# A ninth block in a mixture-of-experts kernel: laying the code behind each "is there a further block?" so that no jump is taken

## The chip, the cores and the metric

The kernel runs on one core of one Trainium2 chip. The time is the device time of one execution in microseconds (us). Five engines run their own instruction streams and meet by semaphores: PE (TensorE, matrix products), DVE (VectorE), ACT (ScalarE), POOL (GpSimd) and SP (SyncE, which here only starts transfers).

## The reference

32 samples of 64 tokens x 256 channels each go through the feed-forward net of one of eight experts, the one that the sample's index names; then come the residual and a layer norm.

```python
Wi_b = Wi[expert_idx]            # 256 x 1024 per sample
Wo_b = Wo[expert_idx]            # 1024 x 256 per sample
h = gelu(einsum('bsh,bhi->bsi', x, Wi_b) + bi_b, exact)
o = einsum('bsi,bih->bsh', h, Wo_b) + bo_b
r = o + x
mu = mean(r); var = mean(square(r - mu))
y = (r - mu) * rsqrt(var + 1e-12) * g_b + be_b
```

With the inputs used the experts have 3, 4, 8, 4, 4, 4, 4 and 1 samples.

## The kernel before

The kernel sorts the samples by expert at run time and works in *blocks* of four samples of one expert (256 tokens). The first eight blocks are one for each expert; an expert with more than four samples gets further blocks behind them. So the number of blocks `n`, read by each engine from a small table (`entry`, L183), lies between `MIN_BLOCKS` = 8 and `MAX_BLOCKS` = 15. Here it is 9: the expert with eight samples has a second block.

For a block, PE multiplies the tokens by the first weights into `preact` (`first_product`, four parts), ACT applies gelu in place and writes the upper half of each number (`h_hi`), DVE the lower half (`h_low`, L602); PE then forms the output sums in `sums_ps` from the halves (`second_product`, four parts: 0 and 1 for the first tile of 128 tokens, 2 and 3 for the second). The weights are split into halves in the same way, `wo_r` for the second ones (ACT L452, DVE `wo_low` L590, in two pieces). Each product of split numbers is three matmuls: L734 or L758, L707 and L708. DVE adds the residual and centres (`centre`, L609 to L615; `centre_last` for the very last tile), ACT sums the squared deviations (`deviations`, L485), POOL takes the root (L376), DVE scales (`finish`, L639), and SP, for the last quarter ACT, stores.

The engines work staggered. PE's step t does the first product of block t between the parts of the second product of block t - 1; DVE's step t holds the second centring of block t - 2 (at its start) and the first of block t - 1. Nothing but each engine's own order and its semaphore waits sets the order of work.

Steps that always occur stand in a row. For the others each engine has a nest of questions: `from_block` (PE and SP) and `with_next` (DVE, ACT, POOL). A question "n > t?" is a compare-and-branch. In before, on yes the code goes on right behind it, with the step of the further block, the next question and all that is nested in it; on no it jumps to the Else part, which holds the end of the work. The Else parts of the inner questions stand ahead of those of the outer ones, so a whole nest lies between a question and its Else. At the end of an Else there is a short jump over the Else parts further out. The questions here are "n > 8?" (yes) and "n > 9?" (no). SP's end (L326) issues the last stores and waits for all of them (L333) ahead of its last jump; behind it lies the exit (DRAIN and semaphore, L60 in the trace), where the engines wait for each other.

Of the kernel before, what the change touches and what calls it, by code (L numbers as in the profile page):

```python
# [18 lines left out]
def expert_ffn(nc, xr, xt, idx, wi, wo, par, out):  # L19
# [13 lines left out]
    MIN_BLOCKS = E  # L33
# [26 lines left out]
    with ctx:  # L60
# [200 lines left out]
        def store(eng, t, slots):  # L261
            rows = samples(eng, t)
            for j in slots:
                eng.wait_ge(y_ready, 2 * t + j // 2 + 1)
                eng.dma_start(out[bass.ds(rows[j], 1), :, :].rearrange("o s h -> (o s) h"), slot(t, j)).then_inc(
                    stored[t % X_RING], 16)

        def from_block(eng, n, t, iteration, end):

            if t == MAX_BLOCKS:  # L270
                end(t)
                return
            with eng.If(n > t):
                iteration(t, t + 1)
                from_block(eng, n, t + 1, iteration, end)
                eng.nop()
            with eng.Else():
                end(t)
                eng.nop()

        def with_next(eng, n, t, iteration, end):

            if t + 1 == MAX_BLOCKS:
                iteration(t, False)
                end(t + 1)
                return
            with eng.If(n > t + 1):
                iteration(t, True)
                with_next(eng, n, t + 1, iteration, end)
                eng.nop()  # L290
            with eng.Else():
                iteration(t, False)
                end(t + 1)
                eng.nop()

        @block.sync
        def _(sp):
# [39 lines left out]
            for t in range(1, MIN_BLOCKS - 2):  # L337
                iteration(t, True)
            from_block(sp, n, MIN_BLOCKS, lambda t, _: iteration(t - 2, True), end)

        @block.gpsimd
        def _(pool):
# [55 lines left out]
            for t in range(MIN_BLOCKS - 1):  # L398
                iteration(t, True)
            with_next(pool, n, MIN_BLOCKS - 1, iteration, end)  # L400

        @block.scalar
        def _(act):
# [118 lines left out]
            for t in range(MIN_BLOCKS - 1):  # L522
                iteration(t, True)
            with_next(act, n, MIN_BLOCKS - 1, iteration, end)

        @block.vector
        def _(dve):
# [149 lines left out]
            for t in range(MIN_BLOCKS - 1):  # L677
                iteration(t, True)
            with_next(dve, n, MIN_BLOCKS - 1, iteration, end)

        @block.tensor
        def _(pe):
# [89 lines left out]
            for t in range(MIN_BLOCKS):  # L772
                iteration(t, True)
            from_block(pe, n, MIN_BLOCKS, iteration, end)


# [30 lines left out]
```

## Time and profile before

| | us |
|---|---|
| median of 3 runs | 131.44 (130.99 to 132.53) |
| the profiled execution's own time | 131.33 |
| its span, first to last instruction | 129.4 |
| PE busy | 114.2 (88%) |
| DVE busy | 100.3 (78%) |
| ACT busy | 96.2 (74%) |
| POOL busy | 69.3 (54%) |

The profile is one execution. Times in it count from the start of its span. A "q" behind an engine's name means its sequencer, which carries out waits, jumps and the issue of transfers.

### The profile page before, as it was taken

How to read it: one execution, taken by the hardware profiler on the slowest of the kernel's cores; microseconds unless marked ns; L12 is line 12 of the kernel's file. 1: busy time of each engine (PE TensorE's matmuls, PEld its weight loads, DVE VectorE, ACT ScalarE, POOL GpSimd, SP SyncE). 2: the span in 40 equal slices, each digit the busy share in tenths (PEclk: the TensorE clock that was granted, in tenths of full speed). 3: DMA queues.
4: the chain of work that ended last, by engine and by line, in shares of the span. 5: the costliest groups of instructions: out<-in, count | busy, mean ns of one | idle time of the engine just before them, and what ended most of it. 6: DMA issues, size and time to landing. Idle time of an engine off the chain costs nothing.

```text
span 129.4 us, 2750 instructions
## 1 busy us (share of the span) xinstructions
PE 114.2 (88%) x880; PEld 110.6 (85%) x880; DVE 100.3 (78%) x191; ACT 96.2 (74%) x186; POOL 69.3 (54%) x84
## 2 busy tenths in 40 slices
PE   6979960999999999999999999999999996968910
PEld 6758851999999999999999999999999996957900
DVE  3500569959899999989998998999899658946370
ACT  3104399999999899989989998998999638860100
POOL 4041048138298749839883983888398417202220
PEclk9976998599999999999999999999999999999997
DMA  2889999999479939966992997599582210110111
GB/s 72 285 182 372 394 329 401 387 392 372 174 213 403 356 90 363 390 225 196 398 382 72 318 388 271 183 400 352 130 314 77 68 46 3 41 45 5 46 41 41
DMA packets 21144, 29.81 MB, mean 230 GB/s; under 512 B 2112, under 2 KB 11328, under 8 KB 21120
## 3 DMA queue, kind: packets, MB, share of 16 engines
q1 hardware_dynamic: 18208, 23.84, 54.1%
q10 hardware_dynamic: 2048, 3.35, 8.2%
q0 software_dynamic: 864, 2.36, 4.8%
q8 instruction: 9, 0.15, 0.5%
q14 instruction: 15, 0.12, 0.3%
HBM read 27.18 MB, written 2.36 MB: 228 GB/s over the span
## 4 chain that ended last, share of the span: by engine, by line
PE 64%; DVE 14%; issue 7%; DMA 6%; ACT 3%; SPq 2%; POOL 1%; DVEq 0%; POOLq 0%
PE sums_ps L758 12%; PE sums_ps L708 11%; PE sums_ps L707 11%; PE preact L734 9%; PE preact L708 9%; PE preact L707 9%; DMA xT_in<-x_columns 6%; DVE wo_r L590 4%; DVE h_lo L602 3%; DVE wi_lo L584 3%; PE preact L685 2%; DVE r L609 2%; SPq L246 2%; DVE centred L615 1%; POOL rstd L376 1%
## 5 line engine op out<-in xcount | busy, mean ns | idle before, releaser
L758 PE MATMUL sums_ps<-wo_r,h_lo 128*128 128x256 f32 x144 | 41.5, 288 | 6.0 <-DVE wo_r L590 4.5
L708 PE MATMUL sums_ps<-wo_r,h_hi 128*128 128x256 f32 x144 | 41.1, 286 | 0.1
L707 PE MATMUL sums_ps<-wo_r,h_hi 128*128 128x256 f32 x144 | 41.1, 285 | 0.0
L734 PE MATMUL preact<-xT_r,wi_lo 128*128 128x256 f32 x128 | 36.4, 284 | 0.4 <-DVE xT_r L595 0.4
L707 PE MATMUL preact<-xT_r,wi_hi 128*128 128x256 f32 x128 | 36.1, 282 | 0.0
L708 PE MATMUL preact<-xT_r,wi_hi 128*128 128x256 f32 x128 | 36.0, 281 | 0.0
L758 PEld LDWEIGHTS sums_ps<-wo_r,h_lo 128*128 128x128 f32 x144 | 27.6, 192 | 6.7 <-issue 5.2
L468 ACT ACTIVATE preact<-preact,params 128x256 f32<-128x256 f32 x64 | 25.8, 441 | 3.1 <-PE preact L708 3.0
L708 PEld LDWEIGHTS sums_ps<-wo_r,h_hi 128*128 128x128 f32 x144 | 27.7, 192 | 0.3 <-issue 0.3
L707 PEld LDWEIGHTS sums_ps<-wo_r,h_hi 128*128 128x128 f32 x144 | 27.6, 192 | 0.0
L258 POOL DMA_INDIRECT xs<-x_rows,row_of x18 | 21.1, 1175 | 9.2 <-issue 9.1
L366 POOL TENSOR_TENSOR xs<-xs,params 128x256 f32<-128x256 f32 x18 | 18.9, 1068 | 12.6 <-DMA params<-vectors 7.7
L584 DVE TENSOR_TENSOR wi_lo<-wi_in,wi_hi 128x1024 fp32r<-128x1024 f32 x16 | 20.4, 1273 | 6.7 <-ACT wi_hi L434 6.7
L602 DVE TENSOR_TENSOR h_lo<-preact,h_hi 128x512 fp32r<-128x512 f32 x36 | 24.6, 682 | 0.8 <-ACT h_hi L477 0.6
L734 PEld LDWEIGHTS preact<-xT_r,wi_lo 128*128 128x128 f32 x128 | 24.2, 189 | 0.8 <-DVE xT_r L595 0.8
L707 PEld LDWEIGHTS preact<-xT_r,wi_hi 128*128 128x128 f32 x128 | 24.2, 189 | 0.0
L708 PEld LDWEIGHTS preact<-xT_r,wi_hi 128*128 128x128 f32 x128 | 24.1, 188 | 0.0
L376 POOL TENSOR_TENSOR rstd<-var_eps,minus_half 128x1 f32<-128x1 f32 x18 | 21.4, 1190 | 3.5 <-DVE var_eps L630 2.0
L373 POOL TENSOR_SCALAR var_eps<-deviation 128x1 f32<-128x1 f32 x17 | 6.5, 380 | 29.9 <-ACT squares L485 29.7
L477 ACT ACTIVATE h_hi<-preact 128x512 fp32r<-128x512 f32 x36 | 21.6, 600 | 1.1
L590 DVE TENSOR_TENSOR wo_r<-wo_in,wo_r 128x1024 fp32r<-128x1024 f32 x18 | 21.9, 1215 | 0.3 <-ACT wo_r L452 0.3
L452 ACT ACTIVATE wo_r<-wo_in 128x1024 fp32r<-128x1024 f32 x18 | 18.9, 1051 | 0.0
(67 smaller groups left out, 109.7 us busy)
## 6 DMA issues: line engine op xcount, KB each, us to landing
wo_in<-w_out SPq DMA_DIRECT2D x8, 1024.0 KB
wi_in<-w_in SPq DMA_DIRECT2D x7, 1024.0 KB, 8.5
params<-vectors SPq DMA_DIRECT2D x9, 388.0 KB, 6.8
y_rows<-xs SPq DMA_DIRECT2D x35, 64.0 KB, 2.2
xT_in<-x_columns SPq DMA_DIRECT2D x34, 64.0 KB, 5.9
wi_in<-w_in ACTq DMA_DIRECT2D x4, 512.0 KB, 5.3
wo_in<-w_out ACTq DMA_DIRECT2D x2, 512.0 KB, 8.9
xs<-x_rows,row_of POOLq DMA_INDIRECT x18, 5.8
```

The lines of the kernel that those rows point to most:

```text
L258: pool.indirect_dma_start(xs[:, t % X_RING, tile, :], None, xr.rearrange("o s h -> (o s) h"), rows_of(t, tile)).then_inc(x_loaded[t % X_RI ...
L366: nc.gpsimd.tensor_tensor(xs[:, t % X_RING, tile, :], xs[:, t % X_RING, tile, :], row(0, t), ALU.add).then_inc(xs_ready, 1)
L376: nc.gpsimd.tensor_tensor(rstd[:, tile:tile + 1], var_eps[:, tile:tile + 1], minus_half[:, :], ALU.pow).then_inc(rstd_ready, 1)
L468: done = nc.scalar.activation(to, pre, ACT.Gelu, bias=bias[:, c:c + 1])
L477: nc.scalar.activation(h_hi[:, t % 2, 2 * q:2 * q + 2, :].rearrange("p c n -> p (c n)"), preact[:, q, :], ACT.Copy).then_inc(h_hi_done, 1)
L584: nc.vector.tensor_tensor(flat(wi_lo, t % 2, wi_piece(piece)), flat(wi_in, t % WI_RING, wi_piece(piece)), flat(wi_hi, t % 2, wi_piece(piec ...
L590: nc.vector.tensor_tensor(wo_r[:, t % 2, a:b, 1, :], wo_in[:, t % WO_RING, a:b, :], wo_r[:, t % 2, a:b, 0, :].bitcast(FP32), ALU.subtract) ...
L602: nc.vector.tensor_tensor(lo, preact[:, q, :], hi.bitcast(FP32), ALU.subtract).then_inc(h_lo_done, 1)
L707: nc.tensor.matmul(columns, weight, parts[:, 0, :], start=False, stop=False)
L708: return nc.tensor.matmul(columns, weight, parts[:, 1, :], start=False, stop=stop)
L734: nc.tensor.matmul(columns, wi_lo[:, t % 2, c, k, :], xT_r[:, t % 2, k, 0, :], start=(k == 0), stop=False)
L758: nc.tensor.matmul(columns, h_lo[:, t % 2, c, tokens], wo_r[:, t % 2, c, 0, :], start=(c == 0), stop=False)
```

## The change

For the first question behind the minimum (n > 8) nothing changes. From the next one on the question is put the other way round: "n < t + 1?", and what stands right behind it is the end of the work; the further block and the nest of questions stand in the Else. The same holds for `with_next`, where the short part is the step without a successor and the end. The work of each branch is the same.

```diff
         def from_block(eng, n, t, iteration, end):
 
             if t == MAX_BLOCKS:
                 end(t)
-                return
-            with eng.If(n > t):
-                iteration(t, t + 1)
-                from_block(eng, n, t + 1, iteration, end)
-                eng.nop()
-            with eng.Else():
-                end(t)
-                eng.nop()
+            elif t == MIN_BLOCKS:
+                with eng.If(n > t):
+                    iteration(t, t + 1)
+                    from_block(eng, n, t + 1, iteration, end)
+                    eng.nop()
+                with eng.Else():
+                    end(t)
+                    eng.nop()
+            else:
+                with eng.If(n < t + 1):
+                    end(t)
+                    eng.nop()
+                with eng.Else():
+                    iteration(t, t + 1)
+                    from_block(eng, n, t + 1, iteration, end)
+                    eng.nop()
...
         def with_next(eng, n, t, iteration, end):
 
             if t + 1 == MAX_BLOCKS:
                 iteration(t, False)
                 end(t + 1)
...
+            else:
+                with eng.If(n < t + 2):
+                    iteration(t, False)
+                    end(t + 1)
+                    eng.nop()
+                with eng.Else():
+                    iteration(t, True)
+                    with_next(eng, n, t + 1, iteration, end)
+                    eng.nop()
```

The rows below are those of the order of instructions, in which plain semaphore waits and register moves have no row; row numbers in the text count an engine's rows from its stream's start. The first place is DVE at its question "n > 9?", row 145 in both kernels. Before, the step for a further block stands behind it, and the code for exactly nine blocks begins at row 444:

```order
L287 COMPARE_AND_BRANCH
L609 SCALAR_TENSOR_TENSOR r,total<-sums_ps,xs 128x256
L612 TENSOR_SCALAR less_mean<-total 128x1
L615 SCALAR_TENSOR_TENSOR centred<-r,less_mean,params 128x256
L602 TENSOR_TENSOR h_lo<-preact,h_hi 128x512
L590 TENSOR_TENSOR wo_r<-wo_in,wo_r 128x4x256
L584 TENSOR_TENSOR wi_lo<-wi_in,wi_hi 128x1024
...
L287 UNCONDITIONAL_BRANCH
L609 SCALAR_TENSOR_TENSOR r,total<-sums_ps,xs 128x256
L612 TENSOR_SCALAR less_mean<-total 128x1
L615 SCALAR_TENSOR_TENSOR centred<-r,less_mean,params 128x256
```

After, the step without a successor stands right behind the question (no `wi_lo`), and its end is the jump in row 176:

```order
L305 COMPARE_AND_BRANCH
L627 SCALAR_TENSOR_TENSOR r,total<-sums_ps,xs 128x256
L630 TENSOR_SCALAR less_mean<-total 128x1
L633 SCALAR_TENSOR_TENSOR centred<-r,less_mean,params 128x256
L620 TENSOR_TENSOR h_lo<-preact,h_hi 128x512
L608 TENSOR_TENSOR wo_r<-wo_in,wo_r 128x4x256
L620 TENSOR_TENSOR h_lo<-preact,h_hi 128x512
...
L657 SCALAR_TENSOR_TENSOR xs<-centred,rstd,params 128x256
L305 UNCONDITIONAL_BRANCH
L627 SCALAR_TENSOR_TENSOR r,total<-sums_ps,xs 128x256
```

With nine blocks DVE used to jump from row 145 to 444; now it goes straight on, and jumps at row 176, behind its last work, to row 470 and from there over the code for eight blocks to the end. ACT, POOL and PE are laid in the same way.

The second place is the end of SP's stream. Before, the last stores for nine blocks end in row 555, reached by a jump from row 164; row 556 jumps over the code for exactly eight blocks (557 to 589) to the exit:

```order
L273 COMPARE_AND_BRANCH
L197 TENSOR_LOAD table
...
L273 UNCONDITIONAL_BRANCH
L189 TENSOR_LOAD table
...
L265 DMA y_rows<-xs 64x256
L277 UNCONDITIONAL_BRANCH [waits stored4,stored5,stored3,stored1,stored2,stored0]
L273 UNCONDITIONAL_BRANCH
L189 TENSOR_LOAD table
```

After, those stores stand behind the question in row 164:

```order
L282 COMPARE_AND_BRANCH
L189 TENSOR_LOAD table
...
L265 DMA y_rows<-xs 64x256
L282 UNCONDITIONAL_BRANCH [waits stored4,stored5,stored3,stored1,stored2,stored0]
L197 TENSOR_LOAD table
...
L285 UNCONDITIONAL_BRANCH [waits stored4,stored5,stored3,stored1,stored2,stored0]
L285 UNCONDITIONAL_BRANCH x5
L274 UNCONDITIONAL_BRANCH
L189 TENSOR_LOAD table
```

The jump that carries the last wait for the stores stands at row 197 and leads to row 552, over the code for ten to fifteen blocks; 552 jumps on to the exit.

## Rows read from the trace of the kernel before

**Rows 1.** The page: busy time of each engine, the chain by engine
```profile
PE 114.2 (88%) x880; PEld 110.6 (85%) x880; DVE 100.3 (78%) x191; ACT 96.2 (74%) x186; POOL 69.3 (54%) x84
...
PE 64%; DVE 14%; issue 7%; DMA 6%; ACT 3%; SPq 2%; POOL 1%; DVEq 0%; POOLq 0%
```

**Rows 2.** Timeline, 102 to 109 us: start, us, engine, line, [idle before, releaser]
```profile
102.27 0.29 PE L708 MATMUL sums_ps<-wo_r,h_hi 128*128 128x256 f32 x1
...
104.84 0.42 DVE L609 SCALAR_TENSOR_TENSOR r<-sums_ps,xs 128x256 f32<-128x256 f32 x1 [2.47 <-issue]
...
105.50 0.51 ACT L485 ACTIVATE squares<-r,less_mean 128x256 f32<-128x256 f32 x1 [2.88 <-DVE less_mean L612]
...
106.50 1.22 DVE L590 TENSOR_TENSOR wo_r<-wo_in,wo_r 128x1024 fp32r<-128x1024 f32 x1
...
106.56 0.28 PE L708 MATMUL preact<-xT_r,wi_hi 128*128 128x256 f32 x1
...
107.87 0.36 PE L758 MATMUL sums_ps<-wo_r,h_lo 128*128 128x256 f32 x1 [1.03 <-DVE wo_r L590]
```

**Rows 3.** DVE, ACT: the question, the first instruction behind it (ns, start us)
```profile
L287 DVEq COMPARE_BRANCH  x1: 67/67/67, 101.9 to 101.9; - x1
L287 ACTq COMPARE_BRANCH  x1: 50/50/50, 102.0 to 102.0; - x1
...
L607 DVEq EVENT_SEMAPHORE  x1: 21/21/21, 104.8 to 104.8; - x1
...
L484 ACTq EVENT_SEMAPHORE  x1: 17/17/17, 104.8 to 104.8; - x1
```

**Rows 4.** Instruction packets, 102.9 to 103.0 us, then 105.4 to 105.6
```profile
q14 instruction: 2, 0.02, 61.7%
...
q14 instruction: 2, 0.02, 22.7%
```

**Rows 5.** PE: its question; its instruction packets, 117.1 to 117.3 us
```profile
L273 PEldq COMPARE_BRANCH  x1: 3482/3482/3482, 113.0 to 113.0; - x1
...
q8 instruction: 1, 0.02, 37.4%
```

**Rows 6.** Timeline, 114.5 to 120 us, of PE and DVE
```profile
114.97 0.28 PE L708 MATMUL sums_ps<-wo_r,h_hi 128*128 128x256 f32 x1
...
115.36 0.42 DVE L609 SCALAR_TENSOR_TENSOR r<-sums_ps,xs 128x256 f32<-128x256 f32 x1 [1.80 <-PE sums_ps L708]
...
116.62 0.36 PE L758 MATMUL sums_ps<-wo_r,h_lo 128*128 128x256 f32 x1 [1.37 <-DVE r L609]
...
117.02 1.22 DVE L590 TENSOR_TENSOR wo_r<-wo_in,wo_r 128x1024 fp32r<-128x1024 f32 x1
...
118.39 0.36 PE L758 MATMUL sums_ps<-wo_r,h_lo 128*128 128x256 f32 x1
...
119.30 0.28 PE L707 MATMUL sums_ps<-wo_r,h_hi 128*128 128x256 f32 x1
...
119.67 0.39 PE L708 MATMUL sums_ps<-wo_r,h_hi 128*128 128x256 f32 x1
```

**Rows 7.** SP: its question, the first instruction behind it (ns, start us)
```profile
L273 SPq COMPARE_BRANCH  x1: 53/53/53, 92.9 to 92.9; - x1
...
L189 SPq TENSOR_LOAD <-table x1: 311/311/311, 98.0 to 98.0; - x1
```

**Rows 8.** SP at the end: last wait, two jumps, exit (ns, start us)
```profile
L279 SPq EVENT_SEMAPHORE  x1: 1596/1596/1596, 126.9 to 126.9; - x1
...
L277 SPq COMPARE_BRANCH  x1: 43/43/43, 128.5 to 128.5; - x1
...
L273 SPq COMPARE_BRANCH  x1: 38/38/38, 128.7 to 128.7; - x1
...
L60 SPq DRAIN  x1: 55/55/55, 129.1 to 129.1; - x1
L60 SPq EVENT_SEMAPHORE  x1: 17/17/17, 129.3 to 129.3; - x1
```

More of the change, by code:

```diff
@@ L285, in with_next @@
                 end(t + 1)
[L286 to L294, printed above, removed]
+            elif t + 1 == MIN_BLOCKS:
+                with eng.If(n > t + 1):
+                    iteration(t, True)
[7 more added lines that the diff above has]
+                with eng.If(n < t + 2):
+                    iteration(t, False)
+                    end(t + 1)
+                    eng.nop()
+                with eng.Else():
+                    iteration(t, True)
+                    with_next(eng, n, t + 1, iteration, end)
+                    eng.nop()
         @block.sync
```

## Prediction

> **What bounds the kernel now.** I read the page first: PE is busy for 114.2 of 129.4 us and carries 64% of the chain that ended last, DVE 14%, and 7% is "issue", time in which an engine waited for nothing that the profile shows [rows 1]. An edit that only moves code can change nothing but such issue time and PE's idle time, so I looked for both behind the questions. The eight experts make nine blocks with these inputs (one expert has eight samples, the others at most four), so "more than 8?" is answered yes and "more than 9?" no. In before the no of the second question is a jump over the code of six further blocks, on each engine.
>
> *DVE and ACT.* DVE asks at 101.9 and executes its next instruction at 104.8; ACT asks at 102.0 and goes on at 104.8 [rows 3]. That is 2.9 and 2.8 us for one jump. What DVE goes on to is the residual sum of block 6 (L609), with 2.47 us idle ahead of it and "issue" as the reason [rows 2]. PE had handed over that sum long before: its last matmul for it starts at 102.27 [rows 2]. In the same stretch two packets of the instruction queue start at 102.9 to 103.0 us, and two more at 105.4 to 105.6 [rows 4]: the code at the far end was not on the engine, was fetched after the jump, and its continuation after the landing.
>
> *PE.* Its sequencer runs ahead of its array, asks at 113.0 and sits in that instruction for 3.48 us [rows 5]. The last matmul of block 7 starts at 114.97, the first one behind the jump at 116.62 [rows 6]. The timeline names DVE's sum as the releaser; that sum frees only the second token tile, and the matmul at 116.62 writes the first, so the jump is what ended last.
>
> *SP.* It asks at 92.9 and goes on at 98.0, 5.1 us later [rows 7], with a 1 MB weight load issued just ahead. Nothing on the chain waits for it there. At the end SP waits for the last stores, 1.6 us from 126.9, takes a jump at 128.5 and a second at 128.7, and reaches its exit at 129.1 and 129.3 [rows 8]. Both of these jumps are short, at most over the code for exactly eight blocks.
>
> **The change part by part.** No instruction of the work is added or removed; the order of work is the same on each engine. What changes is where the taken jumps are.
>
> *Removed, DVE and ACT behind block 7's step.* DVE can take the sum once PE's matmuls are done. Elsewhere it starts 0.39 us behind the start of PE's last matmul (114.97 to 115.36, [rows 6]), so here at 102.27 + 0.39 = 102.66, not 104.84: 2.18 us earlier. The work behind it follows in the same order: DVE's low half of the second weights (L590) starts at 104.3, not 106.50, and ends by 105.5. PE wants that half right behind its matmul of 106.56, and gets it only for 107.87, with 1.03 us idle [rows 2]. Start to start that is 1.31 us where matmuls follow each other at 0.12 us (for instance 118.39 to 119.30 with seven between, [rows 6]). So PE gains 1.31 - 0.12 = **1.19 us**. The other 1.0 us of DVE's 2.18 is slack. ACT's wait of 2.88 us for DVE's mean [rows 2] goes with it, and its own jump of 2.8 us, which lay inside that wait, too.
>
> *Removed, PE behind block 8's step.* The first matmul of the last output product could start 1.5 us earlier (116.62 less 114.97 and 0.12). The second group, at 118.39, waits for the other weight half, which DVE starts at 117.02 and which takes 1.22 us, until 118.24 [rows 6]; DVE began that run at 115.36 on PE's finished sum, before PE was through the jump. So this jump is hidden behind DVE and its removal gives **0**. If DVE's run were shorter it would give up to 1.5 us; what is late next is the weight half in either case. But the jump has a second effect: one more packet of PE's instruction queue starts at 117.1 to 117.3 [rows 5], and at 119.67 a matmul comes 0.37 us behind its predecessor of 119.30 [rows 6]. I read this as code behind the landing that arrived late. Falling through, it arrives in its turn: **0.25 us** gained, 0 if my reading is wrong.
>
> *Removed, SP and POOL.* SP's 5.1 us go, but the stores there feed nothing but the ring of six, and POOL's jump comes while it waits for ACT's deviations in any case: 0. If SP's stores had been late for the ring, POOL's loads would show it; there are none left to make after block 8.
>
> *Sum up to the last store:* -1.19 - 0.25 = -1.44 us, on DVE, ACT and PE alike, since the tail (sum, deviations, root, scale, store) follows PE's last matmul one by one. Bounds: -1.19 to -2.2 (DVE's whole gain).
>
> *Added: the last block's code is now the first branch, so its end jumps over the code of six further blocks.* In before this end lay one short jump from the exit. On SP the new jump spans 355 rows of the order of instructions (197 to 552); the one that cost 5.1 us in before spans 359 (164 to 523). PE, DVE, ACT and POOL get such a jump too, but each has done its last work before the last store lands at 128.5 [rows 8], so their jumps run ahead of SP's. SP takes it *after* its wait for the last stores, and all engines wait for SP. Nothing hides it. Price: no row shows a far jump with idle DMA queues. Below lies the short jump, 0.2 us from 128.5 to 128.7 [rows 8]; above lies SP's own 5.1 us. The nearest are DVE's 2.9 and ACT's 2.8, with light DMA traffic; SP's 5.1 came behind a full megabyte of weights, and at the end the queues are empty. I take 2.85, less the 0.2 that the short jump cost: **+2.65 us**.
>
> *Added, possibly: the code behind the exit.* The profiled execution took 131.33 us for a span of 129.4, so 1.93 us lie around it. DVE's and ACT's landings at 104.8 are followed by packets 0.6 to 0.8 us later [rows 3, 4], so what stands behind SP's landing is not there yet. From packet to use it takes 1.9 us (102.9 to 104.8), so that code is usable some 2.6 us behind the landing, and SP wants it after 0.8 (128.5 to 129.3, [rows 8]): up to 1.8 us late, an estimate. Whether that falls inside the measured time no row shows. Between 0 and 1.8 I take 0.4, near the lower end, since the span itself does not contain it.
>
> **Sum:** 131.33 - 1.44 + 2.65 + 0.4 = 132.94 us. The profiled execution lies 0.11 below the median of 131.44, which runs from 130.99 to 132.53; I say **133.0 us**.
>
> [...] In before, far jumps cost 2.8 to 5.1 us [rows 3, 7]. [...]
>
> **The rivals.** *Faster: the last jump costs nothing.* The condition is that the far code is on SP already, for instance fetched in its 1.6 us of waiting. For it: every other jump in the program gets cheaper. Against: ACT and DVE waited the full time though they too had idle stretches, and SP can't know its target before it executes the jump. It decides if the price falls below 1.44. Time: 131.44 - 1.44 = 130.0. Chance 14%.
>
> *Slower still: the code behind the exit counts in full.* 133.0 + 1.4 = 134.4. Chance 18%.
>
> *The gain does not come.* DVE's earlier start meets another wait, ACT's first activations of block 8, and PE stays at 107.87; against it, these depend on PE's own product, ready at 104. Time: 131.44 + 2.65 + 0.4 = 134.5. Chance 8%.
>
> *Gain and loss cancel*, since with idle queues the fetch is quicker: a price of 1.4 gives 131.4. Chance 10%. That the code is not moved as said is excluded by the order of instructions.
>
> **How the numbers follow.** The forecast (132.4 to 133.6) has 50%. One per cent, about what a measurement of this kernel can tell from no change, is 1.3 us: 130.1 to 132.75. Of the forecast's 50% some 33 lie above 132.75 and 17 below. Slower: 33 + 18 + 8 = 59%. Same: 17 + 10 = 27%. Faster: 14%. The range leaves out the faster rival and the top of the slower ones: 131.2 to 134.5.
>
> **What the profile after would show.** DVE's sum of block 6 at about 102.7 and no "issue" idle there; PE's idle of 1.03 us gone; PE from block 7 to block 8 without a gap at the question, but then about 1.9 us idle before the second group; SP's last wait ending at about 127.1 (128.5 - 1.44); and between the start of SP's last jump pair and its exit some 3.3 us where 0.6 stood. If that last gap is short the prediction is wrong on the fast side; if the span has grown by 1.2 and the time by 2.5 or more, the code behind the exit counted.

## The result, and the profile after

The changed kernel takes 134.36 us in the median of 4 runs (134.22 to 134.99); the kernel before 131.22 in the runs beside it. The ratio is 1.0262, with a 95% interval of 1.0193 to 1.0332: **slower by 2.6%**, where 133.0 us, 1.2% over the median shown before, was forecast. The direction was right; the loss forecast was half of the one that came. A run more than 1.5% above the fastest of the same kernel counts as slow: the ratios here and below leave slow runs out, the medians keep them, and the profiles of three experiments (28 instructions more, DVE and ACT, DVE only) are of slow runs.

The page of the changed kernel: span, busy time of each engine, the instruction packets of the four engines other than PE, and the chain by engine.

```profile
span 132.3 us, 2754 instructions
...
PE 112.2 (85%) x880; PEld 109.9 (83%) x880; DVE 99.8 (75%) x191; ACT 96.6 (73%) x186; POOL 69.2 (52%) x84
...
q14 instruction: 14, 0.11, 0.3%
...
PE 73%; DMA 6%; DVE 4%; ACT 4%; issue 3%; SPq 2%; POOL 1%; DVEq 0%; POOLq 0%
```

The span is 2.9 us longer, PE's busy time is no longer than before [rows 1], and the chain has less "issue" in it (3% for 7%). So the loss is not in the work. The timeline around block 7 and 8, as before (all lines lie 18 further down, so L627 is the old L609, L608 the old L590, L503 the old L485):

```profile
102.52 0.29 PE L726 MATMUL sums_ps<-wo_r,h_hi 128*128 128x256 f32 x1
...
102.92 0.42 DVE L627 SCALAR_TENSOR_TENSOR r<-sums_ps,xs 128x256 f32<-128x256 f32 x1 [0.30 <-PE sums_ps L726]
...
103.58 0.51 ACT L503 ACTIVATE squares<-r,less_mean 128x256 f32<-128x256 f32 x1 [0.72 <-DVE less_mean L630]
...
104.58 1.22 DVE L608 TENSOR_TENSOR wo_r<-wo_in,wo_r 128x1024 fp32r<-128x1024 f32 x1
```

This answers to [rows 2]. DVE takes its sum 0.40 us behind the start of PE's last matmul for it, where it had sat 2.47 us with the reason "issue". ACT's deviations follow at 103.58 and the weight half starts at 104.58; in before they came at 105.50 and 106.50. PE's matmul L758, now L776, has no idle row here any more. At the start of the last output product, the stretch of [rows 6]:

```profile
114.36 0.42 DVE L627 SCALAR_TENSOR_TENSOR r<-sums_ps,xs 128x256 f32<-128x256 f32 x1 [1.80 <-PE sums_ps L726]
...
116.02 1.22 DVE L608 TENSOR_TENSOR wo_r<-wo_in,wo_r 128x1024 fp32r<-128x1024 f32 x1
...
117.38 0.36 PE L776 MATMUL sums_ps<-wo_r,h_lo 128*128 128x256 f32 x1 [1.73 <-DVE wo_r L608]
```

PE passes its question (at 112.0) without a gap and then waits 1.73 us for DVE's weight half, ahead of the second group; the forecast had said about 1.9.

SP's end in the changed kernel answers to [rows 8]: its last wait, the long jump, the short jump, and the exit (duration in ns as min/median/max, then first and last start in us).

```profile
L284 SPq EVENT_SEMAPHORE  x1: 1603/1603/1603, 125.5 to 125.5; - x1
...
L282 SPq COMPARE_BRANCH  x1: 38/38/38, 127.1 to 127.1; - x1
...
L274 SPq COMPARE_BRANCH  x1: 38/38/38, 129.7 to 129.7; - x1
...
L60 ACTq DRAIN  x1: 8/8/8, 128.6 to 128.6; - x1
L60 SPq DRAIN  x1: 58/58/58, 132.0 to 132.0; - x1
L60 SPq EVENT_SEMAPHORE  x1: 17/17/17, 132.2 to 132.2; - x1
```

The last store has landed at 127.1, 1.4 us earlier than in before. Then 2.5 us pass from the long jump to the short one (127.14 to 129.68), and another 2.3 from the short one to DRAIN (129.7 to 132.0), where 0.2 and 0.4 stood in before. The other engines are at the exit long before: ACT, the last of them, at 128.6. The profile lists packets of the kind "instruction" on two queues, q8 (9 packets, 0.15 MB together, about 17 KB each, in both kernels) and q14 (14 packets, 0.11 MB together, about 8 KB each, in the changed one). In before one of q8 starts at 113.94, 0.97 us behind PE's jump of 112.97; of q14 two start at 102.94, behind DVE's jump of 101.91 and ACT's of 102.02, one at 101.62, behind POOL's of 100.32, and one at 96.33, behind SP's of 92.92. In the changed kernel, which takes none of these jumps, q14 has no packet from 87.5 to 98.5 us nor from 98.6 to 124.6, and q8 none from 98.7 to 118.8. I therefore read q8 as PE's and q14 as that of the other four. The place where an engine goes on behind a jump is called its landing here. The packets that matter in the two gaps start at 127.9 to 128.3 us (two, of which one may be another engine's) and at 130.2 to 130.3; one more, at 129.3, follows ACT's landing of 128.4:

```profile
q14 instruction: 2, 0.02, 11.0%
...
q14 instruction: 1, 0.01, 35.4%
```

**The wait for the second packet is what the forecast had too small.** The target of the short jump behind the landing lies in a packet of its own; that packet starts 0.55 us behind the landing, and SP waits for it in full, inside the span.

### The profile page after: what moved, and what is told of

Same layout as the page of the kernel before. It is cut to its first block, busy times and chain, and to the rows that moved or that the text cites. A ratio compares the mean times of both kernels' runs of the same rounds, so it can differ in the third digit from the quotient of the medians.

```text
span 132.3 us, 2754 instructions
## 1 busy us (share of the span) xinstructions
PE 112.2 (85%) x880; PEld 109.9 (83%) x880; DVE 99.8 (75%) x191; ACT 96.6 (73%) x186; POOL 69.2 (52%) x84
## 4 chain that ended last, share of the span: by engine, by line
PE 73%; DMA 6%; DVE 4%; ACT 4%; issue 3%; SPq 2%; POOL 1%; DVEq 0%; POOLq 0%
PE sums_ps L776 13%; PE sums_ps L726 12%; PE sums_ps L725 12%; PE preact L752 11%; PE preact L726 11%; PE preact L725 11%; DMA xT_in<-x_columns 6%; PE preact L703 2%; DVE wo_r L608 2%; SPq L246 2%; ACT preact L486 1%; POOL rstd L394 1%; ACT h_hi L495 1%; ACT wo_r L470 1%; ACT wi_hi L452 1%
## 5 line engine op out<-in xcount | busy, mean ns | idle before, releaser
L776 PE MATMUL sums_ps<-wo_r,h_lo 128*128 128x256 f32 x144 | 41.2, 286 | 5.2 <-DVE wo_r L608 5.2
L776 PEld LDWEIGHTS sums_ps<-wo_r,h_lo 128*128 128x128 f32 x144 | 27.5, 191 | 5.6 <-issue 5.6
L486 ACT ACTIVATE preact<-preact,params 128x256 f32<-128x256 f32 x64 | 25.8, 441 | 3.7 <-PE preact L726 3.5
L384 POOL TENSOR_TENSOR xs<-xs,params 128x256 f32<-128x256 f32 x18 | 19.9, 1128 | 12.4 <-DMA params<-vectors 7.5
L258 POOL DMA_INDIRECT xs<-x_rows,row_of x18 | 20.0, 1111 | 9.5 <-issue 9.4
L602 DVE TENSOR_TENSOR wi_lo<-wi_in,wi_hi 128x1024 fp32r<-128x1024 f32 x16 | 19.8, 1240 | 6.0 <-ACT wi_hi L452 6.0
L608 DVE TENSOR_TENSOR wo_r<-wo_in,wo_r 128x1024 fp32r<-128x1024 f32 x18 | 21.9, 1217 | 0.5 <-ACT wo_r L470 0.5
```

The costliest lines, as they stand in the source:

```text
L258: pool.indirect_dma_start(xs[:, t % X_RING, tile, :], None, xr.rearrange("o s h -> (o s) h"), rows_of(t, tile)).then_inc(x_loaded[t % X_RI ...
L384: nc.gpsimd.tensor_tensor(xs[:, t % X_RING, tile, :], xs[:, t % X_RING, tile, :], row(0, t), ALU.add).then_inc(xs_ready, 1)
L486: done = nc.scalar.activation(to, pre, ACT.Gelu, bias=bias[:, c:c + 1])
L608: nc.vector.tensor_tensor(wo_r[:, t % 2, a:b, 1, :], wo_in[:, t % WO_RING, a:b, :], wo_r[:, t % 2, a:b, 0, :].bitcast(FP32), ALU.subtract) ...
L776: nc.tensor.matmul(columns, h_lo[:, t % 2, c, tokens], wo_r[:, t % 2, c, 0, :], start=(c == 0), stop=False)
```

## The experiments

All kernels compute the whole result. In the experiments by engine both forms of the nest stand side by side; `from_block_yes` and `with_next_yes` are the nest of the kernel before. The same code ahead of the questions ends at different times from run to run (see the end). So the table gives for each profiled execution also two stretches that start at DVE's question "n > 9?": one to SP's first jump behind its last wait, which holds the gain, and one to SP's exit, which holds gain and loss. They are taken from the trace at its full resolution, so they can differ by 0.1 from the rounded times.

| kernel, changed nest on | median, us | ratio to before (95%) | DVE's question to SP's jump behind its last wait, us | DVE's question to exit, us |
|---|---|---|---|---|
| before (none) | 131.22 | | 26.6 | 101.9 to 129.3: 27.4 |
| after (all five) | 134.36 | 1.026 (1.019 to 1.033) | 25.0 | 102.2 to 132.2: 30.0 |
| all but SP | 130.20 | 0.989 (0.983 to 0.995) | 24.9 | 101.6 to 127.8: 26.3 |
| SP only | 136.52 | 1.038 (1.032 to 1.044) | 26.6 | 103.2 to 134.6: 31.4 |
| all five, 58 instructions more | 131.57 | 1.004 (0.999 to 1.009) | 25.0 | 101.2 to 129.2: 28.0 |
| all five, 28 instructions more | 133.74 | 1.016 (1.011 to 1.021) | 25.0 | 103.3 to 133.2: 29.9 |
| all but SP and ACT | 130.14 | 0.991 (0.987 to 0.995) | 25.0 | 101.7 to 127.5: 25.8 |
| DVE and ACT | 130.98 | 0.991 (0.985 to 0.997) | 25.2 | 103.0 to 129.6: 26.6 |
| DVE only | 130.55 | 0.989 (0.984 to 0.995) | 25.4 | 101.9 to 128.1: 26.2 |
| PE only | 131.14 | 1.000 (0.995 to 1.004) | 26.3 | 103.2 to 130.3: 27.1 |

The first stretch repeats well: 25.0 in all three kernels with all five engines changed, 26.6 in both kernels in which the other four are as before. The median of before was 131.47 beside the first four experiments and 131.68 beside the last four.

### All but SP

```diff
-            from_block(sp, n, MIN_BLOCKS, lambda t, _: iteration(t - 2, True), end)
+            from_block_yes(sp, n, MIN_BLOCKS, lambda t, _: iteration(t - 2, True), end)
```

> SP alone keeps the nest of the kernel before; PE, DVE, ACT and POOL have the changed one. Theory (SP's two jumps behind its last wait carry the whole loss): from SP's last wait to its exit 0.6 us as before, the gain of 1.4 us stays, so 131.2 - 1.4 = 129.8 us. Rival (the long jumps of the other engines at their ends hold the exit too, or slow it): their jumps end before the last store lands, so if they matter the time stays above 131 us.

Measured: 130.20 us, faster than before by 1.1%. The loss was SP's. The forecast of 129.8 was 0.4 us too low, and the rival was half right, on a smaller scale than it said: SP's jump at 126.4 (L323) and its DRAIN at 127.0 are as quick as in before, but the exit itself comes only at 127.8.

```profile
L323 SPq COMPARE_BRANCH  x1: 43/43/43, 126.4 to 126.4; - x1
...
L305 ACTq COMPARE_BRANCH  x1: 38/38/38, 124.8 to 124.8; - x1
...
L296 ACTq COMPARE_BRANCH  x1: 38/38/38, 127.5 to 127.5; - x1
...
L60 SPq DRAIN  x1: 55/55/55, 127.0 to 127.0; - x1
L60 ACTq DRAIN  x1: 8/8/8, 127.7 to 127.7; - x1
L60 SPq EVENT_SEMAPHORE  x1: 17/17/17, 127.8 to 127.8; - x1
```

ACT takes its own long jump at 124.8, behind the issue of its store, lands at 127.5 and reaches the exit at 127.7. With SP's loss gone it is ACT that the others wait for, by 0.6 us. So of the engines' late jumps each counts as far as it ends behind the others.

### SP only

```diff
-            from_block(pe, n, MIN_BLOCKS, iteration, end)
+            from_block_yes(pe, n, MIN_BLOCKS, iteration, end)
...
-            with_next(dve, n, MIN_BLOCKS - 1, iteration, end)
+            with_next_yes(dve, n, MIN_BLOCKS - 1, iteration, end)
```

(the same for ACT and POOL)

> SP alone has the changed nest, the other four keep that of the kernel before. Theory: no gain ahead of the last store, and SP's two late jumps cost 2.4 and 1.85 us: 131.2 + 4.25 = 135.5 us. Rival (the loss belongs to the other engines): about 131.2 us.

Measured: 136.52 us; from the question to the exit 4.0 us more than before, against 4.25 expected. Both of SP's jumps wait again, with none of the other engines jumping at that time:

```profile
L282 SPq COMPARE_BRANCH  x1: 38/38/38, 129.8 to 129.8; - x1
...
L274 SPq COMPARE_BRANCH  x1: 38/38/38, 132.3 to 132.3; - x1
...
L60 SPq DRAIN  x1: 58/58/58, 134.4 to 134.4; - x1
```

From the long jump to the short one 2.5 us, from there to DRAIN 2.1. DVE, ACT and POOL have reached the exit by 128.3, so the packets of q14 behind that are SP's own. The one at 130.7 starts 0.9 us behind the long jump, the one at 132.8 starts 0.55 us behind the landing (windows 130.6 to 130.8 and 132.8 to 132.9 us):

```profile
q14 instruction: 1, 0.01, 13.1%
...
q14 instruction: 1, 0.01, 30.2%
```

The rival, a loss of the other engines, has fallen.

### The exit moved within its packet

The waits below stand in code that only ten or more blocks reach, so nothing of them runs; two of them make one instruction. They push the landing of the long jump and the exit behind it further on.

```diff
                 with eng.Else():
+                    if eng.engine == nc.sync.engine and t == MIN_BLOCKS + 1:
+                        for _ in range(116):
+                            eng.wait_ge(samples_ready, 1)
                     iteration(t, t + 1)
```

An *edge* is the place in SP's code where one packet ends and the next begins. The theory tested is that the short jump waits because an edge lies between the landing and its target. Its wait was priced at 1.85 us, the 2.30 from jump to DRAIN in the changed kernel (129.68 to 131.98) less the 0.45 of before (128.67 to 129.12). With landing and target in one packet 134.4 - 1.85 = 132.5 us was expected.

> The changed kernel with 58 wait instructions more in SP's code for ten and more blocks, which is never run here: landing and exit of the last two jumps lie 58 instructions further on. [...] Rival (any jump right behind a landing costs 2.3 us): 134.4 us.

> The same with 28 instructions. Control: if the edge lies at the exit or just ahead of it, as the packets of the kernel before suggest, landing and exit move but landing stays ahead of the edge and exit behind it: 134.4 us, as the changed kernel. If the edge lies just behind the landing, both are in one packet and it takes 132.5 us like the kernel with 58.

Measured: 131.57 us with 58 instructions, 133.74 with 28. SP's long jump, short jump and exit with 58:

```profile
L282 SPq COMPARE_BRANCH  x1: 38/38/38, 126.2 to 126.2; - x1
...
L274 SPq COMPARE_BRANCH  x1: 38/38/38, 128.9 to 128.9; - x1
...
L60 SPq DRAIN  x1: 13/13/13, 129.0 to 129.0; - x1
L60 SPq EVENT_SEMAPHORE  x1: 17/17/17, 129.2 to 129.2; - x1
```

The long jump costs what it did (126.2 to 128.9), the short one nothing: DRAIN follows at 129.0. With 28 the short jump waits 2.1 us as in the changed kernel:

```profile
L274 SPq COMPARE_BRANCH  x1: 38/38/38, 130.9 to 130.9; - x1
...
L60 SPq DRAIN  x1: 58/58/58, 133.0 to 133.0; - x1
```

So it is not the jump right behind a landing that costs, but a target in a packet that is not there. With 58 the packet that starts 0.55 us behind the landing, at 129.4, comes when SP is already through its exit, and nothing waits for it. Counted in the built program, the exit lies 50 instructions behind the landing. Moving both by 28 left the edge of a packet between them, so the edge lies more than 28 instructions behind the landing of the changed kernel; moving them by 58 carried both past it, so it lies 29 to 50 behind. This takes it to be one and the same edge in all three kernels; how many instructions a packet holds no run shows.

The median with 28 came out 0.7 us under the 134.4 that was expected, but its stretch from question to exit is that of the changed kernel (29.9 for 30.0). The median with 58 came out 0.9 us under the expected 132.5; from question to exit it is 2.0 less than in the changed kernel, for 1.85 expected. The rest lies ahead of the questions, where the code is the same; no run shows why. Against before the kernel with 58 gains nothing (1.004): the long jump still takes back what the early jumps give.

### All but SP and ACT

```diff
-            with_next(act, n, MIN_BLOCKS - 1, iteration, end)
+            with_next_yes(act, n, MIN_BLOCKS - 1, iteration, end)
```

on top of the kernel with SP as before.

> SP and ACT keep the nest of the kernel before; PE, DVE and POOL have the changed one. In the kernel with SP alone as before, ACT's own long jump, from 124.8 to 127.5, ends 0.6 us behind SP's arrival at the exit. Theory: with it gone the exit comes 0.6 us earlier, while ACT's jump behind block 7 (2.8 us at 102) is absorbed, since PE needs nothing of block 8's activations before block 8's own output product: 129.6 us. Rival (ACT's early jump now delays block 8, where it had lain under DVE's): 130.5 us or more.

Measured: 130.14 us, ratio 0.991. ACT now reaches the exit at 125.2, and SP's DRAIN is followed by the exit at once:

```profile
L60 ACTq DRAIN  x1: 378/378/378, 125.2 to 125.2; - x1
L60 SPq DRAIN  x1: 55/55/55, 127.3 to 127.3; - x1
L60 SPq EVENT_SEMAPHORE  x1: 17/17/17, 127.5 to 127.5; - x1
```

From question to exit it is 0.5 us shorter than with ACT's nest changed, for 0.6 expected, and the medians (130.20 and 130.14) don't separate the two. ACT's jump behind block 7 is there again, with 1.96 us idle, and is absorbed: DVE's sum of block 7 is still released by PE.

```profile
104.37 0.51 ACT L531 ACTIVATE squares<-r,less_mean 128x256 f32<-128x256 f32 x1 [1.96 <-issue]
...
108.19 0.42 DVE L655 SCALAR_TENSOR_TENSOR r<-sums_ps,xs 128x256 f32<-128x256 f32 x1 [0.48 <-PE sums_ps L754]
```

### DVE and ACT, DVE only, PE only

The edits are the same call replaced for the engines not named.

> DVE and ACT alone have the changed nest. Theory: the 1.19 us of PE's stall come back, ACT's long jump at its end holds the exit by some 0.6 us as in the kernel with SP alone as before: 131.3 - 1.19 + 0.6 = 130.7 us; PE still waits behind its question. Rival (PE's jump is on the path after all and takes the gain back): 131.3 us or more.

Measured: 130.98 us; 0.8 us less than before from question to exit, and 1.4 less up to SP's jump behind its last wait: ACT's long jump at the end takes back the rest. The rival has fallen.

> DVE alone has the changed nest. Theory (of all early jumps DVE's alone is on the path): the full 1.19 us, and no long jump at ACT's end: 130.1 us. Rival (ACT's jump of equal length lies behind DVE's and takes its place): ACT's deviations and activations start at 105 in either case and PE's gain is lost: 131.3 us.

Measured: 130.55 us, ratio 0.989; 1.2 us less than before from question to exit, as expected (1.19). ACT's jump does not take the place of DVE's. PE still has its own jump here:

```profile
115.50 0.36 PE L804 MATMUL sums_ps<-wo_r,h_lo 128*128 128x256 f32 x1 [1.64 <-issue]
...
115.64 1.22 DVE L636 TENSOR_TENSOR wo_r<-wo_in,wo_r 128x1024 fp32r<-128x1024 f32 x1
...
118.45 0.39 PE L754 MATMUL sums_ps<-wo_r,h_hi 128*128 128x256 f32 x1 [0.26 <-issue]
```

It idles 1.64 us ahead of 115.50 and nothing comes of it: the next group starts at 117.01, 0.15 us behind the end of DVE's half of 115.64, as it does in before (118.39 for 118.24). This idle row names "issue" where [rows 6] named DVE's sum, which bears out that there too the jump ended last. The late packet of PE is here as well, starting at 116.09: the matmul at 118.45 starts 0.53 us behind its predecessor, so 0.4 us are lost in this trace, where before lost 0.25. DVE's 1.2 us and these 0.4 add up to the 1.6 us that all five changed nests give.

> PE alone has the changed nest. Theory: its jump behind block 8 is hidden under DVE's run to the second weight half, so only the 0.25 us of the late instruction packet come back: 131.1 us, with the matmul group at 118.4 unmoved. Rival (PE's 3.5 us count): 129.9 us or less.

Measured: 131.14 us, ratio 1.000 (0.995 to 1.004). From question to exit 0.3 us less than before, as expected for the packet alone. PE's jump is gone, and its idle time stands ahead of the second group instead, together with the stall behind DVE's jump:

```profile
109.19 0.36 PE L804 MATMUL sums_ps<-wo_r,h_lo 128*128 128x256 f32 x1 [1.10 <-DVE wo_r L636]
...
118.36 1.22 DVE L636 TENSOR_TENSOR wo_r<-wo_in,wo_r 128x1024 fp32r<-128x1024 f32 x1
...
119.72 0.36 PE L804 MATMUL sums_ps<-wo_r,h_lo 128*128 128x256 f32 x1 [1.73 <-DVE wo_r L636]
```

The 1.10 us at 109.19 answer to the 1.03 of [rows 2], and the 1.73 us at 119.72 are where the 1.37 of [rows 6] went: PE waits about as long one group later. That group is unmoved, as expected: 16.56 us behind DVE's question, for 16.48 in before.

## Why the prediction was right and wrong

*Which jumps are on the path:* right. DVE's jump alone gives 1.2 us, for a term of 1.19. PE's gives 0, and its late packet 0.3 for 0.25 (0.4 once DVE's jump is gone). ACT's early jump gives nothing that shows: up to SP's jump behind its last wait it is 25.0 us with ACT as before and 24.9 with ACT changed, SP being as before in both. POOL's was not tried alone. SP's early 5.1 us were worth nothing, as said: with SP as before and all others changed the gain stands (24.9, for 25.0 with SP changed too).

*The gain up to the last store:* 1.44 us by the sum. SP's last wait ends at 127.1 for 128.5, 1.4 earlier; counted from DVE's question the changed kernel needs 25.0 us and before 26.6, so 1.6. The terms hold.

*The long jump of SP at the end:* 2.65 was forecast above the short one's cost; measured 2.5 from jump to jump (127.14 to 129.68) less 0.2, so 2.4. The row taken, DVE's and ACT's, was the right neighbour, and SP's own 5.1 us behind a megabyte of weights the wrong one. (In before its packet starts at 96.3, 3.4 us behind the jump of 92.9, where DVE's of 102.9 and those of SP's jumps at the end start 0.9 to 1.0 us behind. That the load held it up is likely, but no run leaves the load out.) The first rival, a free last jump, has fallen in four kernels: whenever SP has the changed nest, 2.5 to 2.7 us pass there. Nor was the code fetched during SP's wait for the last stores: with SP alone changed no packet of q14 starts from 109.1 to 130.6 us, and the one of 130.7 starts 0.9 us behind the jump.

*The code behind the landing:* **this is the step that failed.** I had priced a full wait for the packet behind the landing at up to 1.8 us and took 0.4 of it, because I placed that code behind the exit, outside the span. It lay ahead of the exit: the short jump's target, 50 instructions on, was across a packet's edge, and the jump cost 2.3 us for the 0.4 of before, 1.9 net, inside the span. The prediction's own sign says the same: from the start of SP's last jump pair to its exit it expected 3.3 us, and 4.8 passed, although the long jump itself took 0.3 less than its price.

With 1.9 in place of 0.4 the sum is 132.94 + 1.5 = 134.4 us, against 134.36 measured. That this fits to the tenth is partly luck. In the profiled execution the terms are -1.6, +2.4 and +1.85, and DVE's question comes 0.26 us later than in before, which no term had; 131.33 and these give 134.2, and 134.25 was measured. The second rival, with 134.4 us and 18%, names this mechanism and its price; its place was off by one jump.

The trace of before did not speak for 0.4. Its short jump needs 0.4 us to DRAIN [rows 8], where the kernel with 58 instructions more, whose landing and exit share a packet, needs 0.2. And a packet starts at 129.68, 0.56 us behind the DRAIN of before at 129.12, which is the distance measured behind SP's late landings (0.55). I read this now as an edge ahead of the exit in before too, with the packet behind it already there; no run tests that reading.

*What came out better:* laid for each engine by itself, the change is worth having for nine blocks. With the old nest on SP and the new one on the rest the kernel is 1.1% faster than before, and with DVE's alone changed it is too. All runs have nine blocks. With ten or more the changed nest jumps at "n > 9?" and at each further question but the last, where before jumps at the last alone; no run shows what that costs.

## What to carry to other kernels

A taken jump out of the code at hand cost 2.5 to 3.1 us on DVE, ACT and SP in these traces, 3.4 to 4.1 on PE, and 4.9 to 5.1 on SP just behind the issue of a large load. So ask of every branch not how often it is taken but what its engine is doing then: ahead of a wait that it has anyway, a jump was free (PE's: ratio 1.000 without it; SP's: 24.9 us to its last jumps with it, 25.0 without), and behind the last wait of the program each microsecond of it counts (4.0 us more from question to exit with SP alone changed). Lay the code of the case that occurs right behind the question for the engine that others wait for (here DVE), and leave on the engine that closes the program (here SP) the form that jumps early. If a jump must be the last thing, see that its landing and all that follows up to the exit lie in one packet: 58 unused instructions in a branch that is not run took 2.0 us off the stretch from question to exit.

## What was not expected of the hardware

A jump right behind a landing waited a second time, 2.3 us after 2.5, for code only 50 instructions further on; the next packet starts 0.55 us behind SP's late landing in each of the four kernels with the changed nest on SP, never ahead of it. And the part ahead of the questions is less regular than the rest: DVE's question "n > 9?" comes at 101.2 to 103.3 us in ten profiled executions, though in all of them the code ahead of it is the same. The cause is open. For this reason stretches behind a common point tell apart what medians of whole runs barely do.
